# Three second products of the expert FFNs moved to other places in TensorE's order

## The chip, the cores and the metric

One core of a Trainium2 chip runs the whole program in one launch. The metric is the device time of that launch in microseconds (us). The engines are TensorE (PE; PEld is its weight load), VectorE (DVE), ScalarE (ACT), GpSimd (POOL) and SyncE (SP, which issues all DMAs). Each runs its own list of instructions in order and waits on semaphores for the others.

## The reference

The input x has 32 sequences of 256 tokens with 128 features, in fp32. Three layers follow one another, each on a layernorm of its input and added to it:

```python
x = x + 0.5 * ffn(layernorm(x))
x = x + mamba(layernorm(x))
x = x + 0.5 * ffn(layernorm(x))

# ffn: 8 experts, each token takes the one with the largest gate
idx = argmax(softmax(xf @ Wg + bg))
h = gelu(einsum('th,ehi->tei', xf, W1) + b1)     # exact gelu
y = einsum('tei,eih->teh', h, W2) + b2
out = y[token, idx[token]]

# mamba: rmsnorm, in_proj to 2 x 256, causal conv of 4 taps, silu,
# x_proj, dt = softplus(...), a scan over 256 steps with 16 states a channel
h = exp(dt * A) * h + (dt * x) * B ;  y = h . C
out = ((y + D * x) * silu(z)) @ out_proj + residual
```

## The kernel before

**Tiling.** The 8192 tokens are cut into 16 chunks of 512 (two sequences). A chunk goes through the first FFN (called f1, w = 0 in the code), the mamba layer (p) and the second FFN (f2, w = 1). The program is a software pipeline: iterations i = -4 to 18, each of 16 slots. In iteration i the scan works on chunk i, while other stages work on chunk i + off, with off from 4 (its load) to -3 (its store). Every engine has its own list that is written out by hand: tables name the slot, and a place within it, at which each step stands.

**The scan.** A slot handles two units of a chunk, so a chunk has 32. For a unit ACT makes the decay, an Exp into one of three PSUM banks dA (L632); DVE scans over time (L759, or L757 in slots 1, 3, 5, 9 and 14) and multiplies by C (L763; in those five slots POOL does it, L944); POOL makes dt*x*B (L936); PE sums the states into the bank Y (L489). A decay may be made only when the unit three before it has left its dA bank, that is after DVE's product (L763) or scan (L757) of that unit. ACT is one slot ahead: at slot 15 it makes the decays of units 0 and 1 of the next chunk.

**An FFN.** Only the chosen expert's values matter. For each expert e a first product puts xn @ W1 plus a bias that is very negative for tokens that chose another expert into the single PSUM bank PH (L461 in bf16, then L462 in fp32). ACT copies the bank into hs (L597, `take_first`); the next first product can start only after that copy. After the eighth, two gelus run over hs in place (L610, with a table load ahead, and one back at L614). Then for each e a second product adds hs @ W2 into the bank PY (`second_product`, L477: four matmuls of 128x128 in fp32, two records each in the trace; for e = 0 also a bias, L475). When all eight are in, DVE adds PY to X (L815, `add_to_x`), which frees PY for the other FFN.

**Where they stand.** `W1_AT` gives for each first product its slot and place on PE, its slot and place on ACT, and the chunk's offset; `W2_AT` gives slot, place and offset of each second product. On PE a slot runs: stages of place 0 and first products of place 0, stages of place 1, the state sum, then for k = 1, 2, 3 the first and then the second products of place k, then stages of place 2. Of f1, eight first products end in slot 15, the gelus follow on ACT at slot 15.5, and the second products of that chunk stand in slots 4 to 9 of the next iteration. DVE's add of f1 is at its place 10.0, and layernorm statistics for p follow at 10.5 (L738 to L744), POOL's roots (L881 to L901) at 11 and its normalization (L919) at 12, PE's transposes of that (L443) at slot 13, the projections x1 and x0 (L451) at slot 14. ACT's copy of the last but two first products, the taps of the convolution (L647) and DVE's part of it (L776) lie in slots 14 and 15. Of f2, the second products stand in slots 10 to 15; DVE's add of f2 is at place 1.5 of the next iteration. Slots 0 to 3 on PE hold the last state sum, the transposes of f1's layernorm (L443), three first products of f2, the gate (L531) and z0, z1 (L451); then comes the output projection (L511).

Of the kernel before, what the change touches and what calls it, by code (L numbers as in the profile page):

```python
# [68 lines left out]
         [(15, 1, 15, 0, -1), (15, 2, 15, 1, -1), (15, 3, 15, 3, -1), (1, 0, 0, 0, -2), (2, 0, 2, 0, -2),  # L69
          (3, 0, 3, 0, -2), (5, 0, 4, 2, -2), (6, 0, 6, 0, -2)]]  # L70

W2_AT = [[(s, 1, 2) for s in (4, 6, 8, 8, 8, 9, 9, 9)],
         [(s, k, -2) for s, k in ((10, 1), (11, 1), (12, 1), (13, 1), (14, 1), (14, 1), (15, 1), (15, 2))]]
W1_ORDER = sorted((s, k, w, e, off) for w in range(2) for e, (s, k, _, _, off) in enumerate(W1_AT[w]))
W1_TAKES = sorted((s, k, w, e, off) for w in range(2) for e, (_, _, s, k, off) in enumerate(W1_AT[w]))
W1_PLACE = {(w, e): n for n, (_, _, w, e, _) in enumerate(W1_ORDER)}
# [20 lines left out]
def w2_units(s, place):  # L97

    return [(w, e, off) for w in range(2) for e, (at, k, off) in enumerate(W2_AT[w]) if (at, k) == (s, place)]

# [930 lines left out]
```

## Time and profile before

| | us |
|---|---|
| median of 3 runs | 1493.84 (1493.03 to 1496.21) |
| the profiled execution's own time | 1495.2 |
| its span, first to last instruction | 1493.4 |
| PE busy | 1232.2 (83%) |
| POOL busy | 1067.6 (71%) |
| DVE busy | 1061.7 (71%) |
| ACT busy | 874.2 (59%) |
| mean granted TensorE clock | 0.849 of full |

The profiled execution took 1.8 us more than its span, and 1.4 us more than the median. In the middle of the program an iteration takes 82.4 us, and each engine has idle stretches in it at its own places; which engine is last changes within the iteration, so a busy share alone says little. The chain of waits follows the program back from its end through whatever was last at each step.

### The profile page before, as it was taken

What the parts mean: (1) busy time and instruction counts of PE and PEld (TensorE: products, weight loads), DVE (VectorE), ACT (ScalarE), POOL (GpSimd) and SP (SyncE); (2) the same over time, 40 slices, a digit from 0 to 9 for tenths busy, and PEclk for the clock granted to TensorE, in tenths of its full rate; (3) what the DMA queues carried; (4) which work ended last, traced back from release to release, by engine and by line L of the source; (5) the groups of instructions that cost most, each with busy time, mean ns of one, the idle gap of its engine ahead of it and who ended that gap; (6) DMA issues with size and microseconds to landing.
All of it is one profiled execution on the core that took longest, in us unless ns stands there. A gap on an engine that the chain in (4) does not pass through costs nothing.

```text
span 1493.4 us, 16302 instructions
## 1 busy us (share of the span) xinstructions
PE 1232.2 (83%) x5188; PEld 612.7 (41%) x5188; DVE 1061.7 (71%) x1713; ACT 874.2 (59%) x1171; POOL 1067.6 (71%) x900
## 2 busy tenths in 40 slices
PE   2777768889898989989898988899898978667677
PEld 1333314234443534445353444444353434333344
DVE  2022887887878787877878787878878776979910
ACT  0244656476666767575667667575756675474532
POOL 1026796978878788868788787878687886997600
PEclk9989876788888998888888889888888987978786
DMA  3005050413233231503232332305032322232000
GB/s 84 1 0 205 10 198 9 158 43 120 92 108 106 89 111 33 181 23 127 80 120 92 108 106 73 127 24 185 28 115 85 122 85 105 101 114 92 1 7 14
DMA packets 60405, 130.02 MB, mean 87 GB/s; under 512 B 7744, under 2 KB 26864, under 8 KB 52128
## 3 DMA queue, kind: packets, MB, share of 16 engines
q1 hardware_dynamic: 60320, 128.98, 25.1%
q8 instruction: 42, 0.69, 0.2%
q14 instruction: 43, 0.35, 0.1%
HBM read 106.94 MB, written 22.02 MB: 86 GB/s over the span
## 4 chain that ended last, share of the span: by engine, by line
PE 41%; ACT 24%; DVE 23%; issue 8%; POOL 3%; SPq 1%; ACTq 0%; DVEq 0%; DMA 0%; POOLq 0%
PE PH L462 12%; PE PY L477 9%; DVE dA L759 9%; PE G L451 9%; ACT hs L610 6%; ACT dA L632 5%; DVE hb L757 4%; ACT hs L597 4%; DVE hb L763 3%; PE PH L461 3%; ACT L614 3%; ACT L610 2%; PE Y L489 2%; PE G L511 2%; PE G L531 2%
## 5 line engine op out<-in xcount | busy, mean ns | idle before, releaser
L936 POOL TENSOR_TENSOR hb<-dtx_rep,bs 128x1024 f32<-128x1024 f32 x256 | 598.8, 2361 | 0.0
L759 DVE TENSOR_TENSOR_SCAN dA<-dA,hb 128x512 f32<-128x512 f32 x352 | 429.8, 1221 | 68.5 <-ACT dA L632 61.6
L632 ACT ACTIVATE dA<-dt_rep,A 128x512 f32<-128x512 f32 x512 | 342.2, 689 | 143.4 <-DVE hb L763 128.7
L597 ACT COPY hs<-PH 128x512 f32<-128x512 f32 x256 | 149.4, 584 | 388.2 <-PE PH L462 387.9
L462 PE MATMUL PH<-xnT,W 128*128 128x512 f32 x512 | 339.0, 749 | 0.0
L477 PEld LDWEIGHTS PY<-W,hs 128*128 128x128 f32 x2048 | 281.8, 208 | 101.2 <-issue 88.8
L477 PE MATMUL PY<-W,hs 128*128 128x128 f32 x2048 | 323.2, 304 | 0.0
L944 POOL TENSOR_TENSOR hb<-hb,cs 128x1024 f32<-128x1024 f32 x80 | 188.4, 2355 | 140.7 <-DVE hb L757 140.7
L763 DVE TENSOR_TENSOR hb<-dA,cs 128x512 f32<-128x512 f32 x352 | 243.5, 692 | 25.2 <-DVE dA L759 0.9
L757 DVE TENSOR_TENSOR_SCAN hb<-dA,hb 128x512 f32<-128x512 f32 x160 | 186.3, 1206 | 102.6 <-ACT dA L632 99.5
L489 PE MATMUL Y<-hb,Sel 128*32 128x512 f32 x1024 | 164.5, 716 | 19.8 <-POOL hb L944 10.4
L461 PE MATMUL PH<-ohT,Lm 24*128 24x512 bf16 x256 | 109.1, 426 | 83.4 <-ACT hs L597 82.7
L610 ACT ACTIVATE hs<-hs 128x2048 f32<-128x2048 f32 x64 | 121.3, 1909 | 0.4
L462 PEld LDWEIGHTS PH<-xnT,W 128*128 128x128 f32 x512 | 86.6, 212 | 68.3 <-issue 68.3
L461 PEld LDWEIGHTS PH<-ohT,Lm 24*128 24x128 bf16 x256 | 23.5, 92 | 219.7 <-ACT hs L597 147.0
L776 DVE SCALAR_TENSOR_TENSOR xs<-G,Wc,xs 128x506 f32<-128x506 f32 (+2 forms) x96 | 67.2, 742 | 65.0 <-ACT xs L647 62.7
L531 PE MATMUL G<-Wg,xnT 128*128 128x8 f32 x256 | 56.2, 348 | 64.2 <-ACT xnT L590 64.2
L881 POOL TENSOR_SCALAR neg<-mv 128x4 f32<-128x4 f32 x48 | 9.7, 203 | 127.3 <-DVE mv L744 127.3
L963 POOL TENSOR_TENSOR dt<-dt,sp 128x1024 f32<-128x1024 f32 x16 | 37.6, 2353 | 83.5 <-ACT sp L676 83.5
L531 PEld LDWEIGHTS G<-Wg,xnT 128*128 128x128 f32 x256 | 53.8, 309 | 94.3 <-ACT xnT L590 94.0
L489 PEld LDWEIGHTS Y<-hb,Sel 128*32 128x32 f32 x1024 | 22.7, 116 | 114.1 <-issue 86.6
L815 DVE SCALAR_TENSOR_TENSOR X<-PY,X 128x512 f32<-128x512 f32 x32 | 21.8, 682 | 60.8 <-PE PY L477 60.8
(85 smaller groups left out, 1190.7 us busy)
## 6 DMA issues: line engine op xcount, KB each, us to landing
dtx_rep<-dtx_rows SPq DMA_DIRECT2D x32, 1024.0 KB, 6.5
dt_rep<-dt_rows SPq DMA_DIRECT2D x32, 1024.0 KB, 8.2
bs<-bc_rows SPq DMA_DIRECT2D x64, 256.0 KB, 3.7
cs<-bc_rows SPq DMA_DIRECT2D x64, 256.0 KB, 4.5
dtx_rows<-dtx SPq DMA_DIRECT2D x32, 256.0 KB, 2.5
dt_rows<-dt SPq DMA_DIRECT2D x32, 256.0 KB, 2.6
X<-in_x SPq DMA_DIRECT2D x16, 256.0 KB, 3.0
out<-X SPq DMA_DIRECT2D x16, 256.0 KB, 2.4
```

Source lines behind the costliest of these rows:

```text
L461: nc.tensor.matmul(PH[:, :], Lm[:, e, :], ohT[:, w, :], start=True, stop=False)
L462: nc.tensor.matmul(PH[:, :], W1[:, e, :], xnT[:, w, :], start=False, stop=True).then_inc(ph_full, 1)
L477: last = nc.tensor.matmul(PY[:, P * j:P * (j + 1)], hs[:, w, e, P * j:P * (j + 1)], W2[:, e, :], start=False, stop=e == E - 1 and j == J - 1)
L489: last = nc.tensor.matmul(Y[D32 * g:D32 * (g + 1), :], Sel[:, :], hb[:, (2 * k + g // 2) % HR, g % 2], start=q == 0, stop=q == NQ - 1)
L597: nc.scalar.copy(hs[:, w, e, :], PH[:, :]).then_inc(ph_free, 1)
L610: nc.scalar.activation(a, a, ACT.Gelu).then_inc(gelu[w], 1)
L632: nc.scalar.activation(dA[u % NA][:, :], dt_rep[:, h, g, :], ACT.Exp, scale=A[:, h, g, q:q + 1]).then_inc(decay, 1)
L757: nc.vector.tensor_tensor_scan(x_in_hb, a, x_in_hb, 0.0, ALU.mult, ALU.add).then_inc(scan, 1)
L759: nc.vector.tensor_tensor_scan(a, a, x_in_hb, 0.0, ALU.mult, ALU.add).then_inc(scan, 1)
L763: nc.vector.tensor_tensor(x_in_hb, a, cs[:, q, :], ALU.mult).then_inc(prod, 1)
L936: nc.gpsimd.tensor_tensor(hb[:, s % HR], dtx_rep[:, h, 2 * m:2 * m + 2, :], bs[:, q, None, :].broadcast_to([P, 2, CH]), ALU.mult).then_inc ...
L944: nc.gpsimd.tensor_tensor(hb[:, s % HR], hb[:, s % HR], cs[:, q, None, :].broadcast_to([P, 2, CH]), ALU.mult).then_inc(prod_p, 1)
```

## The change

One table changes. It holds for each expert of each FFN the slot, the place and the chunk offset of its second product.

```diff
-W2_AT = [[(s, 1, 2) for s in (4, 6, 8, 8, 8, 9, 9, 9)],
-         [(s, k, -2) for s, k in ((10, 1), (11, 1), (12, 1), (13, 1), (14, 1), (14, 1), (15, 1), (15, 2))]]
+W2_AT = [[(s, k, 2) for s, k in ((4, 1), (6, 1), (8, 1), (8, 1), (8, 1), (9, 1), (9, 1), (9, 3))],
+         [*[(s, 1, -2) for s in (10, 11, 12, 13, 14, 15)], (0, 1, -3), (1, 1, -3)]]
```

Of f2, experts 0 to 3 stay. Slot 14 held two second products (4 and 5) and slot 15 two more (6 and 7); now slot 14 holds expert 4, slot 15 expert 5, and experts 6 and 7 stand in slots 0 and 1 of the next iteration. Of f1, expert 7 moves within slot 9 from ahead of a first product to behind it. No instruction is added or removed, and no engine but PE has another order; the semaphores count on.

PE from x0 (L451) in slot 14 to the last first product of slot 15, in the middle of the program, before. L451 is a projection, L477 second products, L461 with L462 a first product, L489 the state sum:

```order
L451 MATMUL G0<-xrT,Win 128x512
L477 MATMUL PY<-W2,hs 128x128 x8
L461 MATMUL PH<-ohT,Lm 128x512
L462 MATMUL PH<-xnT,W1 128x512
L489 MATMUL Y<-hb,Sel 32x512 x4
L461 MATMUL PH<-ohT,Lm 128x512
L462 MATMUL PH<-xnT,W1 128x512
L477 MATMUL PY<-W2,hs 128x128 x4
L461 MATMUL PH<-ohT,Lm 128x512
L462 MATMUL PH<-xnT,W1 128x512
L477 MATMUL PY<-W2,hs 128x128 x4
L461 MATMUL PH<-ohT,Lm 128x512
L462 MATMUL PH<-xnT,W1 128x512
```

and now:

```order
L451 MATMUL G0<-xrT,Win 128x512
L477 MATMUL PY<-W2,hs 128x128 x4
L461 MATMUL PH<-ohT,Lm 128x512
L462 MATMUL PH<-xnT,W1 128x512
L489 MATMUL Y<-hb,Sel 32x512 x4
L461 MATMUL PH<-ohT,Lm 128x512
L462 MATMUL PH<-xnT,W1 128x512
L477 MATMUL PY<-W2,hs 128x128 x4
L461 MATMUL PH<-ohT,Lm 128x512
L462 MATMUL PH<-xnT,W1 128x512
L461 MATMUL PH<-ohT,Lm 128x512
L462 MATMUL PH<-xnT,W1 128x512
```

Four matmuls of L477 (one second product) are gone ahead of the first PH pair, and no L477 stands any more between the last two pairs.

PE from the last state sum (slot 0) to the gate (L531, slot 2), before:

```order
L489 MATMUL Y<-hb,Sel 32x512 x4
L443 MATMUL G0<-Id,xn 128x128 x4
L461 MATMUL PH<-ohT,Lm 128x512
L462 MATMUL PH<-xnT,W1 128x512
L461 MATMUL PH<-ohT,Lm 128x512
L462 MATMUL PH<-xnT,W1 128x512
L531 MATMUL G1<-Wg,xnT 128x8 x4
```

and now:

```order
L489 MATMUL Y<-hb,Sel 32x512 x4
L477 MATMUL PY<-W2,hs 128x128 x4
L443 MATMUL G0<-Id,xn 128x128 x4
L461 MATMUL PH<-ohT,Lm 128x512
L462 MATMUL PH<-xnT,W1 128x512
L477 MATMUL PY<-W2,hs 128x128 x4
L461 MATMUL PH<-ohT,Lm 128x512
L462 MATMUL PH<-xnT,W1 128x512
L531 MATMUL G1<-Wg,xnT 128x8 x4
```

One second product now stands ahead of the transposes L443, another between the two first products.

PE in slot 9 and on to the gate of f2, before:

```order
L443 MATMUL G1<-Id,xn 128x128 x4
L489 MATMUL Y<-hb,Sel 32x512 x4
L477 MATMUL PY<-W2,hs 128x128 x12
L461 MATMUL PH<-ohT,Lm 128x512
L462 MATMUL PH<-xnT,W1 128x512
L461 MATMUL PH<-ohT,Lm 128x512
L462 MATMUL PH<-xnT,W1 128x512
L531 MATMUL G0<-Wg,xnT 128x8 x4
```

and now:

```order
L443 MATMUL G1<-Id,xn 128x128 x4
L489 MATMUL Y<-hb,Sel 32x512 x4
L477 MATMUL PY<-W2,hs 128x128 x8
L461 MATMUL PH<-ohT,Lm 128x512
L462 MATMUL PH<-xnT,W1 128x512
L477 MATMUL PY<-W2,hs 128x128 x4
L461 MATMUL PH<-ohT,Lm 128x512
L462 MATMUL PH<-xnT,W1 128x512
L531 MATMUL G0<-Wg,xnT 128x8 x4
```

The last of the three second products of slot 9 now follows the first product.

## Rows read from the trace of the kernel before

**Rows 1.** The page: busy time, share of the span, instructions of each engine.

```profile
PE 1232.2 (83%) x5188; PEld 612.7 (41%) x5188; DVE 1061.7 (71%) x1713; ACT 874.2 (59%) x1171; POOL 1067.6 (71%) x900
```

**Rows 2.** Chain of waits, slots 14 to 0: start us, us, what.

```profile
705.52 1.78 PE PY L477 x16
...
711.05 0.89 PE PY L477 x8
...
713.40 0.59 ACT hs L597
```

**Rows 3.** Timeline of ACT, same place: start, duration, what, [idle before, releaser].

```profile
712.02 0.69 ACT L632 ACTIVATE dA<-dt_rep,A 128x512 f32<-128x512 f32 x1 [0.30 <-DVE hb L763]
713.40 0.59 ACT L597 COPY hs<-PH 128x512 f32<-128x512 f32 x1 [0.69 <-PE PH L462]
713.89 0.70 ACT L632 ACTIVATE dA<-dt_rep,A 128x512 f32<-128x512 f32 x1
```

**Rows 4.** Timeline of DVE, slots 14 to 1.

```profile
707.27 2.72 DVE L776 SCALAR_TENSOR_TENSOR xs<-G,Wc,xs 128x506 f32<-128x506 f32 x4 [2.65 <-ACT xs L647]
...
713.10 0.69 DVE L763 TENSOR_TENSOR hb<-dA,cs 128x512 f32<-128x512 f32 x1
...
725.45 0.68 DVE L815 SCALAR_TENSOR_TENSOR X<-PY,X 128x512 f32<-128x512 f32 x1
```

**Rows 5.** Timeline of DVE, then of ACT, where chunk 2's scan begins.

```profile
301.05 0.69 DVE L763 TENSOR_TENSOR hb<-dA,cs 128x512 f32<-128x512 f32 x1
...
301.78 0.69 ACT L632 ACTIVATE dA<-dt_rep,A 128x512 f32<-128x512 f32 x1 [0.60 <-DVE hb L763]
```

**Rows 6.** Timeline of PE, slots 0 to 4.

```profile
718.34 0.38 PE L461 MATMUL PH<-ohT,Lm 24*128 24x512 bf16 x1 [1.18 <-ACT hs L597]
...
722.04 0.60 PE L461 MATMUL PH<-ohT,Lm 24*128 24x512 bf16 x1 [2.27 <-ACT hs L597]
...
735.46 2.02 PE L511 MATMUL G<-Wo,y 128*128 128x128 f32 x16
```

**Rows 7.** Windows: us, busy (count) of PE, PEld, DVE, ACT, POOL; granted clock.

```profile
717.00:721.50 4.50, 1.60 (x5) 0.39 (x3) 2.43 (x3) 4.47 (x5) 2.65 (x2) 1.00 0.00 0
722.00:735.00 13.00, 12.48 (x26) 4.11 (x26) 11.78 (x17) 8.20 (x13) 8.03 (x4) 0.50 0.14 40
```

**Rows 8.** Timeline of PE, then DVE, slots 9 and 10.

```profile
757.22 2.94 PE L477 MATMUL PY<-W,hs 128*128 128x128 f32 x24
...
763.18 0.39 PE L461 MATMUL PH<-ohT,Lm 24*128 24x512 bf16 x1 [1.64 <-ACT hs L597]
...
764.87 0.68 DVE L815 SCALAR_TENSOR_TENSOR X<-PY,X 128x512 f32<-128x512 f32 x1
```

**Rows 9.** Timeline of PE, DVE, POOL, iteration -1.

```profile
134.01 0.66 PE L443 MATMUL G<-Id,xr 128*128 128x128 f32 x4
...
125.94 0.69 DVE L815 SCALAR_TENSOR_TENSOR X<-PY,X 128x512 f32<-128x512 f32 x1 [12.48 <-PE PY L477]
...
132.21 1.75 POOL L919 TENSOR_SCALAR xr<-X,neg,rms 128x128 f32<-128x128 f32 x4
```

**Rows 10.** Timeline of DVE, iteration 0.

```profile
185.81 0.68 DVE L815 SCALAR_TENSOR_TENSOR X<-PY,X 128x512 f32<-128x512 f32 x1
187.66 1.23 DVE L759 TENSOR_TENSOR_SCAN dA<-dA,hb 128x512 f32<-128x512 f32 x1 [1.18 <-ACT dA L632]
```

**Rows 11.** Timeline of POOL, iteration 1.

```profile
273.81 0.20 POOL L881 TENSOR_SCALAR neg<-mv 128x4 f32<-128x4 f32 x1 [0.61 <-DVE mv L744]
```

**Rows 12.** Timeline of DVE, chunk 15's second unit pair.

```profile
1363.05 2.34 DVE L757 TENSOR_TENSOR_SCAN hb<-dA,hb 128x512 f32<-128x512 f32 x2 [0.87 <-ACT dA L632]
```

**Rows 13.** Timeline of PE, iteration 13, where the output projection ran at the low clock.

```profile
1227.82 3.75 PE L511 MATMUL G<-Wo,y 128*128 128x128 f32 x16 [4.12 <-ACT zs L655]
```

**Rows 14.** Chain of waits: the second dt copy of iteration 13, and of iteration 7.

```profile
1247.65 0.69 ACT dt L668
...
749.86 0.69 ACT dt L668
```

## The prediction

> **What bounds the kernel now.** I read the page first. PE is busy for 83% of the span and DVE and POOL for 71% [rows 1], so no engine is full, and the order within an iteration decides. Next the chain of waits, in the middle of the program, where an iteration takes 82.4 us. From slot 14 on it runs over PE, through the second products that the change touches (two of them in 1.78 us, one in 0.89), and leaves for ACT's copy of a first product at 713.40 [rows 2]. Taken alone this says: each second product less ahead of that copy is worth 0.89 us in each iteration. The reader should look at what ACT does after the copy, and at what else it waits for there. After the copy comes the decay of unit 1 at 713.89 [rows 3]. It needs its dA bank back, from a product that DVE began at 713.10 and that takes 0.69 us: free at 713.79 [rows 4]. DVE is thus 0.10 us behind PE as the cause. Where DVE alone is last, at the start of chunk 2, the product ends at 301.05 + 0.69 = 301.74 and the decay starts at 301.78, 0.04 us later [rows 5]. Then the timelines of the engines: where they are idle, and what ends it.
>
> **Slots 14 and 15, removed.** Of the products that leave, one (0.89 us, [rows 2]) stood ahead of the first product whose copy the chain takes, the other behind it. PE gets there 0.89 us sooner. ACT then has only the decay of unit 0 ahead, which DVE frees at 712.02 [rows 3] and the change does not move. The copy starts at about 712.6, and the decay of unit 1 at 713.79 + 0.04 = 713.83 instead of 713.89: 0.06 us, in eleven iterations 0.7 us. DVE itself does not come sooner: its work in these slots hangs on the convolution's taps, for which it was idle 2.65 us [rows 4], and these need only x1, x0 and a copy that all stand ahead of the removed product. Next late after PE is DVE, at once. Bounds of this term: 0.04 us of gain an iteration, and 0.89 if my reading of the bank is wrong (first rival).
>
> **Slots 0 and 1, added.** PE waits for ACT's copies there 1.18 us, and then 2.27 us [rows 6]. The product of expert 6 takes the time that was given free ahead, so the transposes and the next first product (718.34) stand where they were. That of expert 7 starts at about 719.7 and ends at 720.6 at the full clock, ahead of the first product at 722.04. At half the clock (16 such records in 3.75 us, [rows 13]) it takes 1.88 and ends at 721.6, still ahead. Then DVE's add of f2 at 725.45 [rows 4] has its eighth product 4.8 us early. Price: nothing. Without the cover, where no gelu keeps ACT busy, each would cost 0.89.
>
> **Slot 9.** In the middle of the program PE finishes the three second products (2.94 us for three, [rows 8]) and the first product behind them by 761.5, and waits for ACT until 763.18. The exchange leaves both in that stretch; the eighth product ends at 761.5 instead of 760.1, and DVE adds f1 at 764.87 [rows 8]. Nothing. At the start there are no gelus of f2 at that place, and two effects show. (a) DVE's add waits for the eighth product itself: idle 12.48 us until 125.94 [rows 9]. It now comes one first product later, about 1.37 us. Its statistics and POOL's roots follow, POOL's normalization from 132.21 for 1.75 us, and PE's transposes at 134.01 [rows 9] begin as that ends. Iteration -1 loses about 1.3. Iteration -2 has the same path; I take 0.8 for it, between nothing and 1.3. (b) In iterations 0 and 1 DVE waits on ACT behind that first product: idle 1.18 until 187.66 [rows 10]. The first product is done 0.89 sooner; the add (185.81, 0.68 us) moves back by some 0.4, and DVE gains 0.8. In iteration 1 the path goes on over POOL, which had waited only 0.61 us [rows 11]: gain 0.6. Together 1.3 + 0.8 - 0.8 - 0.6 = 0.7 us lost. Bounds: a gain of 1.4 if only (b) holds, a loss of 2.1 if only (a).
>
> **The end.** No f1 is left there, so no gelu covers slots 0 and 1. At the start of chunk 15, DVE was already idle 0.87 us behind ACT [rows 12], and ACT behind a first product that now has the product of expert 6 ahead: 0.8 lost. In iteration 15 PE and ACT alternate on first products and their copies. Expert 6 between the state sum and the next first product costs 0.89 there; in iteration 16 one second product less stands ahead of the first of these and the others fill waits for copies, some 0.75 gained. Together 0.9 lost; bounds 0 and 2.6.
>
> **The sum.** Measured against the profiled execution: -0.7 + 0.7 + 0.9 = +0.9, so 1495.2 becomes 1496.1. This execution took 1.4 us more than the median of the runs (1493.84), so the forecast is 1494.7. A measurement of this kernel can tell about 0.2%, 3 us, from no change.
>
> **The clock.** The windows show PE 1.60 of 4.50 us busy at the full clock, and right behind it 13 us at a granted clock of 0.50, that is 1.2 GHz of 2.4 [rows 7]. The low stretch ends about where the output projection starts at 735.46, which takes 2.02 us for 16 records [rows 6], nearly twice the 0.89 for 8 at the full clock. So the low clock costs nothing now: the path there is DVE's. The product of expert 7 falls into the idle stretch that precedes the fall. The Trainium skill (TensorE: Matmul & The Clock Gate, what's actually happening) says that throttled is the default and that activity lifts it. By that rule added work there delays the fall. The trace agrees on the order, idle and then low; for how much work suffices it has no row.
>
> **Rivals.**
> 1. *The chain as written.* PE, not DVE, holds the decay of unit 1: 0.89 us in eleven iterations, 9.8 us, less the 1.6 lost at the ends: 1494.7 - 9.1 = 1485.6. For it speaks the chain of waits, which names PE and ACT; against it the 0.04 us of [rows 5] beside the 0.10 here. Or the ends turn out well: expert 6 and 7 between the last first products keep the clock up there, an estimated microsecond each for two or three. Chance of faster by over 0.2%: 0.15.
> 2. *The low clock moves onto the critical stretch.* The fall comes later, and the low stretch reaches past 735.46, over the output projection, the first second products, B, C and dt, where PE sets the pace. One iteration shows the price: in iteration 13 the projection took 3.75 us [rows 13] from 1227.82, and ACT's second dt copy came at 1247.65, 19.83 us after its start. In iteration 7 that is 749.86 - 735.46 = 14.40 [rows 6, 14]. So at most 5.4 us an iteration, 60 us in eleven: 1554. It decides from the point where the low stretch ends behind the start of the projection. Against it: in the low stretch PE is busy 12.48 of 13 us [rows 7] with work that starts when ACT is ready, and stays where it is, so the rise should come where it came. I take four iterations of eleven at two thirds of the price: 14 us, 1508. Chance of slower by over 0.2%: 0.25, with smaller shifts and a loss of 3 us at the ends in it.
> 3. *The change doesn't do what it says*: it does; PE's order shows the three moves and no other.
>
> **How the numbers follow.** No change 0.60, faster 0.15, slower 0.25. The forecast's own range is 1491.5 to 1497. The range for 8 in 10 takes in half of each rival's side: 1488 to 1506.
>
> **What would show it.** Right: the decay of unit 1 follows DVE's product by 0.04 us, iterations stay at 82.3 to 82.4, PE's wait of 1.18 stays, that of 2.27 shrinks to about 1.4, a new one of some 0.9 stands in slot 15, DVE's add of f1 in iteration -1 comes 1.4 us later, in the middle everything stands as before. Wrong: iterations of 81.5 us (rival 1), or a granted clock of 0.50 between the output projection and dt (rival 2).

## The result, and the profile after

The changed kernel takes 1510.3 us (median of 4 runs, 1505.45 to 1511.29); the kernel before took 1493.43 beside it (4 runs, 1492.01 to 1496.21). The ratio is 1.0104, with a 95% interval of 1.0078 to 1.0131: slower by 1%. The forecast was 1494.7 with a range to 1506. Rival 2 had 1508, for a reason that turned out to be about half of it. One of the ten executions of e11 below took 2091.06 us; it is left out of that kernel's ratio, but its median of 1496.04 has it in (1495.47 without it).

The page of the kernel after, busy time of each engine, beside [rows 1]:

```profile
PE 1226.6 (81%) x5188; PEld 613.8 (41%) x5188; DVE 1062.3 (70%) x1713; ACT 874.1 (58%) x1171; POOL 1066.5 (71%) x900
```

The work is the same. PE is even 5.6 us less busy in a span that is 15.6 us longer (1509.0 instead of 1493.4, granted clock 0.859 instead of 0.849). So the sums of busy time don't show the loss, nor does the mean clock, which is higher than before; where the low clock falls has to be looked up stretch by stretch. To do that I cut each span where ACT begins the decay (L632) of a chunk's unit 1. The profiled executions give:

| stretch, us | before | after | difference |
|---|---|---|---|
| start to unit 1 of chunk 0 | 145.01 | 155.97 | +10.96 |
| chunk 0 to chunk 2 | 156.77 | 154.66 | -2.11 |
| chunk 2 to chunk 12, ten iterations | 824.89 | 832.80 | +7.91 |
| chunk 12 to chunk 15 | 231.75 | 230.56 | -1.19 |
| chunk 15 to the end | 134.98 | 135.0 | 0.0 |

**The middle: two iterations of eleven.** Most iterations take 82.35 us, 0.06 less than before. Timelines of DVE and ACT of the kernel after, the counterpart of [rows 3, 4] (start, duration, what, [idle before, releaser]):

```profile
726.10 0.69 DVE L763 TENSOR_TENSOR hb<-dA,cs 128x512 f32<-128x512 f32 x1
```

```profile
725.02 0.69 ACT L632 ACTIVATE dA<-dt_rep,A 128x512 f32<-128x512 f32 x1 [1.20 <-DVE hb L763]
725.65 0.58 ACT L597 COPY hs<-PH 128x512 f32<-128x512 f32 x1
726.82 0.69 ACT L632 ACTIVATE dA<-dt_rep,A 128x512 f32<-128x512 f32 x1 [0.60 <-DVE hb L763]
```

The product ends at 726.10 + 0.69 = 726.79 and the decay of unit 1 starts at 726.82, 0.03 behind it. ACT's copy is early now, and ACT waits 0.60 us for DVE. That is the forecast's reading of the bank.

But iterations 3 and 9 take 86.86 and 86.85 us. Timeline of PE of the kernel after from slot 15 to the projection, first in iteration 7, a usual one:

```profile
726.28 0.38 PE L461 MATMUL PH<-ohT,Lm 24*128 24x512 bf16 x1 [0.87 <-ACT hs L597]
...
734.97 0.39 PE L461 MATMUL PH<-ohT,Lm 24*128 24x512 bf16 x1 [1.38 <-ACT hs L597]
...
738.06 1.88 PE L531 MATMUL G<-Wg,xnT 128*128 128x8 f32 x8 [1.65 <-ACT xnT L590]
...
748.39 2.02 PE L511 MATMUL G<-Wo,y 128*128 128x128 f32 x16 [2.34 <-ACT zs L655]
```

and in iteration 3:

```profile
404.14 1.06 PE L531 MATMUL G<-Wg,xnT 128*128 128x8 f32 x8 [1.65 <-ACT xnT L590]
...
414.47 2.53 PE L511 MATMUL G<-Wo,y 128*128 128x128 f32 x16 [2.98 <-ACT zs L655]
...
417.15 0.80 PE L477 MATMUL PY<-W,hs 128*128 128x128 f32 x2
```

The windows of the same iteration 3 (us, busy (count) of PE, PEld, DVE, ACT, POOL; granted clock, DMA share, GB/s):

```profile
400.00:405.50 5.50, 2.80 (x12) 1.58 (x13) 3.88 (x5) 5.08 (x9) 1.40 (x1) 1.00 0.00 0
405.50:409.20 3.70, 3.70 (x9) 0.74 (x11) 3.53 (x6) 0.69 (x1) 3.70 (x3) 0.54 0.52 142
409.20:415.80 6.60, 3.38 (x22) 1.68 (x18) 6.14 (x10) 5.21 (x8) 4.73 (x3) 1.00 0.01 2
415.80:426.00 10.20, 10.20 (x35) 4.84 (x34) 6.68 (x17) 4.35 (x6) 8.38 (x8) 0.50 0.00 1
```

The reader is to see two low stretches between unit 1 and dt, where the kernel before had one [rows 7]. (Both kernels have a further one later in the iteration; it is not at issue here.) In the kernel before the low stretch of iteration 7 began 7.7 us after unit 1 (721.6 - 713.89). With the product of expert 7 ahead it begins 9.9 us after it in iteration 7 (736.7 - 726.82) and 12.7 in iteration 3 (405.6 - 392.90), where even the gate L531 still runs at full clock (1.06 us instead of 1.88). The clock is back at 1.00 by 409.2. PE is then done early with little work, waits 2.98 us for ACT's z, and the granted clock falls again at 415.8, just as the output projection has begun. The projection itself is not late: it starts 21.57 us after unit 1 in iteration 3 as in iteration 7 and in the kernel before (735.46 - 713.89). From here on PE sets the pace: two records of a second product take 0.80 us (0.49 in iteration 7), and the rest up to 426.0 runs at 1.2 GHz too. ACT's dt copies come at 430.76 and 433.37, that is 40.47 us after the decay of unit 1 for the second of them; in iteration 7 it is 762.78 - 726.82 = 35.96. The difference is 4.5 us, and it is the whole difference of the iteration. The same holds for all profiles of this case: from iteration 3 to 10 the projection takes 2.02 to 2.07 us behind a wait of 2.41 us or less, and 2.51 to 2.85 us behind a wait of 2.98 us, and it is these iterations, and no others, that take 86.9 us.

**The start.** The first add of f1 that is exposed, then the second, in the timeline of DVE, beside [rows 9]; and PE between them:

```profile
81.77 0.69 DVE L815 SCALAR_TENSOR_TENSOR X<-PY,X 128x512 f32<-128x512 f32 x1 [10.51 <-PE PY L477]
...
134.43 0.69 DVE L815 SCALAR_TENSOR_TENSOR X<-PY,X 128x512 f32<-128x512 f32 x1 [16.07 <-PE PY L477]
```

```profile
86.33 1.13 PE L462 MATMUL PH<-xnT,W 128*128 128x512 f32 x2
89.80 0.66 PE L443 MATMUL G<-Id,xr 128*128 128x128 f32 x4 [2.35 <-POOL xr L919]
...
93.21 2.08 PE L451 MATMUL G<-xrT,Win 128*128 128x512 f32 x2 [1.22 <-ACT xrT L590]
...
95.75 2.08 PE L462 MATMUL PH<-xnT,W 128*128 128x512 f32 x2
```

The same place in the kernel before, timeline of PE:

```profile
86.42 1.80 PE L462 MATMUL PH<-xnT,W 128*128 128x512 f32 x2
88.00 1.06 PE L443 MATMUL G<-Id,xr 128*128 128x128 f32 x4
...
92.16 1.12 PE L451 MATMUL G<-xrT,Win 128*128 128x512 f32 x2 [1.22 <-ACT xrT L590]
...
93.53 1.12 PE L462 MATMUL PH<-xnT,W 128*128 128x512 f32 x2
```

Here PE went from the first product to the transposes without a wait. The clock was low for a short time, from 86.7 to 90.1 (the transposes took 1.06 us), and then high until 100.4. Now the add of f1 in iteration -2 comes at 81.77 instead of 79.69, POOL's normalization follows it, and PE waits 2.35 us for POOL. The transposes start at 89.80 instead of 88.00, 1.8 us later; 0.7 of that was there ahead of the exchange (a first product at 76.25 instead of 75.53). They still run at the full clock, but at 91.5 it falls and stays low until 98.4: the same matmuls take 2.08 us instead of 1.12. Windows over the start, after and then before (columns as above):

```profile
92.00:100.00 8.00, 6.79 (x10) 2.16 (x10) 0.78 (x2) 3.01 (x5) 2.73 (x5) 0.60 0.00 0
...
112.00:125.00 13.00, 13.00 (x36) 5.68 (x35) 0.41 (x1) 5.11 (x7) 0.00 (x0) 0.61 0.03 7
```

```profile
92.00:100.00 8.00, 4.73 (x10) 1.45 (x10) 3.80 (x6) 5.04 (x7) 0.79 (x2) 1.00 0.00 0
...
112.00:125.00 13.00, 13.00 (x73) 8.60 (x73) 0.41 (x1) 6.74 (x9) 2.27 (x1) 1.00 0.12 26
```

In the last window PE is busy without a break in both kernels, at 1.00 before and 0.61 after, and gets through 73 records before and 36 after (some of them larger ones). The next low stretch is longer too, 105.2 to 122.3 instead of 100.4 to 110.6, and so is the one behind it, 139.3 to 153.0 instead of 137.9 to 141.3. The loss of 11 us builds up so: the gate of f1 in iteration -2 starts at 108.04 instead of 104.54 (3.5); from there to the add of f1 it takes 26.4 us instead of 21.4 (5.0, of them 1.4 for the first product that the exchange put ahead, the rest is the clock); and from the add to chunk 0's unit 1 21.54 instead of 19.07 (2.5).

### The profile page after: what moved, and what is told of

The parts are those of the page before. It is cut to its first block, busy times and chain, and to the rows that moved or that the text cites. A ratio compares the mean times of both kernels' runs of the same rounds, so it can differ in the third digit from the quotient of the medians.

```text
span 1509.0 us, 16302 instructions
## 1 busy us (share of the span) xinstructions
PE 1226.6 (81%) x5188; PEld 613.8 (41%) x5188; DVE 1062.3 (70%) x1713; ACT 874.1 (58%) x1171; POOL 1066.5 (71%) x900
## 4 chain that ended last, share of the span: by engine, by line
PE 31%; DVE 30%; ACT 23%; issue 10%; POOL 4%; SPq 1%; DVEq 0%; ACTq 0%; DMA 0%; POOLq 0%
DVE dA L759 12%; PE PH L462 8%; PE G L451 7%; PE PY L477 6%; ACT hs L610 6%; ACT dA L632 5%; DVE hb L763 5%; DVE hb L757 5%; ACT hs L597 3%; PE G L511 2%; PE PH L461 2%; DVE xs L776 2%; ACT L614 2%; PE Y L489 2%; ACT L610 2%
## 5 line engine op out<-in xcount | busy, mean ns | idle before, releaser
L632 ACT ACTIVATE dA<-dt_rep,A 128x512 f32<-128x512 f32 x512 | 342.6, 689 | 174.9 <-DVE hb L763 153.6
L477 PEld LDWEIGHTS PY<-W,hs 128*128 128x128 f32 x2048 | 287.3, 209 | 122.7 <-issue 110.0
L462 PE MATMUL PH<-xnT,W 128*128 128x512 f32 x512 | 331.6, 734 | 0.0
L477 PE MATMUL PY<-W,hs 128*128 128x128 f32 x2048 | 331.5, 306 | 0.0
L489 PE MATMUL Y<-hb,Sel 128*32 128x512 f32 x1024 | 164.9, 717 | 28.0 <-POOL hb L944 15.3
L461 PE MATMUL PH<-ohT,Lm 24*128 24x512 bf16 x256 | 108.3, 423 | 76.6 <-ACT hs L597 76.1
L462 PEld LDWEIGHTS PH<-xnT,W 128*128 128x128 f32 x512 | 85.6, 210 | 67.4 <-issue 67.4
L531 PE MATMUL G<-Wg,xnT 128*128 128x8 f32 x256 | 52.0, 332 | 73.7 <-ACT xnT L590 73.6
L461 PEld LDWEIGHTS PH<-ohT,Lm 24*128 24x128 bf16 x256 | 23.5, 92 | 197.3 <-ACT hs L597 125.4
L531 PEld LDWEIGHTS G<-Wg,xnT 128*128 128x128 f32 x256 | 49.0, 286 | 97.8 <-ACT xnT L590 97.8
L489 PEld LDWEIGHTS Y<-hb,Sel 128*32 128x32 f32 x1024 | 22.9, 116 | 121.4 <-issue 87.7
```

The costliest lines, as they stand in the source:

```text
L461: nc.tensor.matmul(PH[:, :], Lm[:, e, :], ohT[:, w, :], start=True, stop=False)
L462: nc.tensor.matmul(PH[:, :], W1[:, e, :], xnT[:, w, :], start=False, stop=True).then_inc(ph_full, 1)
L477: last = nc.tensor.matmul(PY[:, P * j:P * (j + 1)], hs[:, w, e, P * j:P * (j + 1)], W2[:, e, :], start=False, stop=e == E - 1 and j == J - 1)
L489: last = nc.tensor.matmul(Y[D32 * g:D32 * (g + 1), :], Sel[:, :], hb[:, (2 * k + g // 2) % HR, g % 2], start=q == 0, stop=q == NQ - 1)
L632: nc.scalar.activation(dA[u % NA][:, :], dt_rep[:, h, g, :], ACT.Exp, scale=A[:, h, g, q:q + 1]).then_inc(decay, 1)
```

## Experiments

The ratio is of each kernel to the kernel before in the same rounds. The same kernel varies by up to 12 us between executions (before: 1485.63 to 1497.75 in 31); a profile shows one of them. So profiles are compared here by stretches. Chunk 0's unit 1 stands at 144.7 to 147.5 us in the eight profiled kernels whose start is that of the kernel before. Where a kernel's profiled execution is far from its median, this is said.

### Each part alone

**e1_f1_only**: only the exchange in slot 9 (the first changed line of the diff).

> Only the exchange in slot 9 (f1, expert 7 behind the first product); f2 as before. Theory A (the exchange costs at the start: DVE's add of f1 comes later in iterations -2 and -1, PE idles ahead of the transposes of the p layer and runs at the low clock after it): chunk 0's unit 1 starts 9 to 11 us later than the 145.0 us of before, the middle has iterations of 82.4 us as before, total 1502 to 1505. Rival B (all of the loss comes from the f2 part): total within 2 us of before, 1493.

Measured: 1501.24 us (before 1494.93), ratio 1.0038 (1.0012 to 1.0065). Chunk 0's unit 1 at 156.97, iterations 3 to 10 at 82.41, iteration 11 at 84.31 (83.12 before). The exchange costs at the start what the whole change costs there, a little more than expected, and nothing in iterations 3 to 10.

**e2_f2_only**: only the three moves of f2 (the second changed line).

> Only the f2 part (experts 5, 6, 7 in slots 15, 0 and 1); f1 as before. Theory A: the start is as before (unit 1 of chunk 0 at about 145 us), iterations take 82.35 us but for some (2 of 11 in the changed kernel) with 4.5 us more, in which the low-clock stretch reaches past the output projection; total 1497 to 1503. Rival B: 1508 to 1511. Rival C (nothing in the middle, that was chance): 1493 to 1494.

Measured: 1501.01 us, ratio 1.0045 (1.0025 to 1.0066). Chunk 0's unit 1 at 147.24. Iteration 5 takes 86.87 us, its second dt copy again 40.47 after unit 1, and iteration 11 takes 84.19; the others from 3 to 10 take 82.35. Iteration 11 can't be put down to this move, since e1 has 84.31 there without it. From chunk 12 to 15 it takes 230.82 us.

**e5_f1_from_2**: the exchange in slot 9 from iteration 2 on.

```diff
                         for unit in w2_units(s, k):
-                            second_product(it, *unit)
+                            if (s, k) != (9, 3) or it.i0 >= 2:
+                                second_product(it, *unit)
+                        if (s, k) == (9, 1) and it.i0 < 2:
+                            second_product(it, 0, 7, 2)
```

> The exchange in slot 9 from iteration 2 on only; iterations -2 to 1 and all of f2 are as before. Theory A (the f1 part costs only at the start, where DVE's add waits for the eighth product itself): no loss, 1492 to 1496, unit 1 of chunk 0 at about 145 us. Rival (it costs in the middle too): 1498 or more.

Measured: 1492.6 us (before 1492.64), ratio 0.9997 (0.9984 to 1.0011). The exchange is free wherever the gelus of f2 stand; what it costs, it costs in the iterations before 2.

**e10_f2_chunks_to_10** and **e11_f2_chunks_from_11**: the moves of f2 for the first eleven chunks alone, or for the last five alone. The first of them (the other has `chunk >= 11`):

```diff
+            def moved(chunk):
+                return chunk <= 10
...
-                        for unit in w2_units(s, k):
-                            second_product(it, *unit)
+                        for w, e, off in w2_units(s, k):
+                            if w == 0 or e < 5 or not moved(it.i0 + off):
+                                second_product(it, w, e, off)
+                        for at, e, off in ((15, 5, -2), (0, 6, -3), (1, 7, -3)):
+                            if (s, k) == (at, 1) and moved(it.i0 + off):
+                                second_product(it, 1, e, off)
```

> The move of the three second products of f2 for chunks 0 to 10 alone; chunks 11 to 15 and f1 stand as before. Theory (in the middle the product of expert 7 in PE's idle stretch puts the fall of the clock off, and in some iterations it then falls a second time ahead of the output projection, 4.5 us each, while 0.06 us is gained in each): one to three iterations of 86.9 us between chunks 3 and 11, all others 82.35, and from chunk 12 on the spans of the kernel before: in all +2 to +8 us, 1495 to 1501. Rival (the loss of f2's move comes from the end alone): no iteration over 82.7, 0.5 us faster than before.

Measured: 1499.87 us (before 1492.69), ratio 1.0049 (1.0030 to 1.0068). Iteration 5 takes 86.85 us and iteration 11 84.15, the others 82.33 to 82.35 up to there; behind them iteration 13 takes 82.46 with its second dt copy at 38.63 instead of 35.68, as it also happens in the kernel before. The rival (loss from the end alone) is out. The loss is as large as that of e2, where f2 is moved for all chunks (1.0045).

> The move of the three second products of f2 for chunks 11 to 15 alone; chunks up to 10 and f1 stand as before. Theory (at the end the product of expert 6 stands ahead of a first product that ACT waits for, and one product less in slot 14 leaves PE idle and its clock low): everything as before until chunk 11, then 0 to 4 us slower, 1493 to 1497; DVE waits over 1 us for ACT's decay at the start of chunk 14 or 15. Rival (the loss comes from the middle alone; at the end the first products at full clock gain as much as expert 6 costs): 1488 to 1493.

Measured: 1496.04 us, ratio 1.0018 (0.9990 to 1.0046): the interval holds 1, so the time alone doesn't decide. The trace does: the middle stands as before, and iteration 14 takes 70.73 us, where the nine profiled kernels with the old order at the end have 66.9 to 69.0 (e12 not counted, which adds work there). Timeline of DVE and PE in e11, where chunk 14's scan begins:

```profile
1296.22 2.34 DVE L764 TENSOR_TENSOR_SCAN hb<-dA,hb 128x512 f32<-128x512 f32 x2 [1.27 <-ACT dA L639]
```

```profile
1288.43 0.38 PE L461 MATMUL PH<-ohT,Lm 24*128 24x512 bf16 x1 [1.66 <-ACT hs L604]
1288.74 1.81 PE L462 MATMUL PH<-xnT,W 128*128 128x512 f32 x2
1290.48 1.94 PE L489 MATMUL Y<-hb,Sel 128*32 128x512 f32 x8
1292.35 1.20 PE L477 MATMUL PY<-W,hs 128*128 128x128 f32 x8
1293.48 0.38 PE L461 MATMUL PH<-ohT,Lm 24*128 24x512 bf16 x1
```

and the same place in e8 (below), which has the old order here:

```profile
1284.55 0.38 PE L461 MATMUL PH<-ohT,Lm 24*128 24x512 bf16 x1
1284.86 1.12 PE L462 MATMUL PH<-xnT,W 128*128 128x512 f32 x2
1285.92 1.06 PE L489 MATMUL Y<-hb,Sel 128*32 128x512 f32 x8
1286.91 0.39 PE L461 MATMUL PH<-ohT,Lm 24*128 24x512 bf16 x1
```

From one first product to the next it is 2.36 us in e8 and 5.05 in e11. Of these 2.69, the product of expert 6 takes 1.13; the rest is the low clock behind a wait of 1.66 us, in L462 (0.69 more) and in L489 (0.88 more). The wait is for a copy of ACT that itself comes no later than in e8. PE is there sooner, since one second product less stands in slot 14, and the one that stood between these two first products (1283.56 in e8, 1.05 us) is gone.

**e3_f2_both_in_slot0**: the moves of f2 with experts 6 and 7 both in slot 0, so that none stands in the idle stretch.

```diff
-         [(s, k, -2) for s, k in ((10, 1), (11, 1), (12, 1), (13, 1), (14, 1), (14, 1), (15, 1), (15, 2))]]
+         [*[(s, 1, -2) for s in (10, 11, 12, 13, 14, 15)], (0, 1, -3), (0, 1, -3)]]
```

> As e2, but experts 6 and 7 of f2 both in slot 0; between the two first products of slots 1 and 2 PE is idle again as before. If the product in that idle stretch is what moves the low-clock stretch, no iteration of the middle takes over 83 us here, and the total is 1493 to 1496. If it is the work taken from slots 14 and 15, it is as e2.

Measured: 1496.17 us, ratio 1.0032 (1.0009 to 1.0055). No iteration of the middle over 82.7 us in the profiled execution (1495.8), and chunk 12 to 15 in 230.3. Its runs reach from 1492.8 to 1502.9, so this one profile doesn't show that the others had no long iteration. It fits the theory and doesn't prove it. Nor do the ratios: the intervals of e2 and e3 overlap.

### The clock alone

**e4_idle_filled_before**: the kernel before, no product moved; four matmuls of 128x128 are added where the change put expert 7. Their result is not read.

```diff
                         first_product(it, *unit)
+                    if s == 1 and it.has(0):
+                        it.wait_free(pe, g_free, "gate_f1")
+                        for j in range(J):
+                            nc.tensor.matmul(G[1][:, P * j:P * (j + 1)], W1[:, 7, :], W2[:, 7, :],
+                                             start=True, stop=True)
```

> The kernel before, with four matmuls of 128x128 more in slot 1 of every iteration from 0 on, written to the bank of the gate ahead of the gate, which overwrites them. They lie in the idle stretch in which expert 7 lies in the changed kernel, and no table is changed. Theory A (activity there moves the low-clock stretch): some iterations of the middle have 4.5 us more, total 1498 to 1504. If it is the order of the second products and not PE's activity: 1493 to 1494.

Measured: 1498.86 us, ratio 1.0040 (1.0018 to 1.0061). Iterations 5 and 10 take 86.9 us. Windows of iteration 5 of this kernel:

```profile
560.80:564.20 3.40, 3.40 (x5) 0.60 (x3) 3.26 (x4) 0.69 (x1) 3.40 (x3) 0.50 0.55 154
564.20:571.00 6.80, 3.58 (x21) 1.61 (x21) 6.31 (x12) 5.02 (x7) 4.94 (x3) 1.00 0.00 1
571.00:581.30 10.30, 10.30 (x36) 5.21 (x36) 6.70 (x16) 4.53 (x7) 8.31 (x7) 0.50 0.01 2
```

This is iteration 3 of the changed kernel again, with nothing moved and nothing needed in the added work; the projection starts 21.58 us after unit 1 as elsewhere. So the 4.5 us come from the clock, and work in the idle stretch is enough to bring them about.

**e6_f1_start_filled**: e1 with eight matmuls more ahead of the transposes for p in iterations -2 and -1, in the wait for POOL. Their result is overwritten.

```diff
                 if now("ln_p"):
+                    if it.i0 in (-2, -1):
+                        it.wait_free(pe, g_free, "ln_p")
+                        fill(G[G_AT["ln_p"][0]], 8)
                     it.wait(pe, xr_ready, 2, 1, 1)
...
+            def fill(bank, n):
+                for j in range(n):
+                    nc.tensor.matmul(bank[:, P * (j % J):P * (j % J + 1)], W1[:, 7, :], W2[:, 7, :],
+                                     start=True, stop=True)
```

> As e1 (the f1 part alone), with eight matmuls of 128x128 more ahead of the p layer's transposes in iterations -2 and -1, in the stretch in which PE waits for POOL there (2.35 us in the changed kernel). They write a bank that the transposes overwrite. If most of the 11 us at the start is the low clock that follows this stretch: unit 1 of chunk 0 at 147 to 150 us, total 1493 to 1497. If it is the direct delay of DVE's add and what follows: as e1, 156 to 157 us, or later, total 1501.

Measured: 1490.8 us (before 1492.64), ratio 0.9987 (0.9976 to 0.9999), where e1 had 1.0038: some 7.5 us. Chunk 0's unit 1 stands at 144.55 instead of 156.97, in an execution that was 5 us faster than the median. Timeline and windows of this kernel at the start:

```profile
86.51 1.95 PE L553 MATMUL G<-W 128*128 128x128 f32 x16
89.03 0.66 PE L443 MATMUL G<-Id,xr 128*128 128x128 f32 x4 [0.57 <-POOL xr L928]
```

```profile
92.00:100.00 8.00, 4.73 (x10) 1.45 (x10) 3.68 (x6) 5.04 (x7) 1.97 (x5) 1.00 0.00 0
...
112.00:125.00 13.00, 13.00 (x72) 8.48 (x71) 0.41 (x1) 6.87 (x9) 2.26 (x1) 1.00 0.09 26
```

The exchange is still there, and so is its direct delay; the wait of 2.35 has become 0.57, the clock stays at 1.00 until 100.3, and the loss is gone. So most of the loss at the start goes with the low clock. How much exactly isn't shown: time and unit 1 are both better than expected, and the fill may gain something in the kernel before too, which no run tried alone. A hint is e9 below, which has such fill in addition to that of e8, with unit 1 at 139.42 instead of 142.77.

### A kernel that beats both

**e7_end_filled**: the kernel before with fill in iteration 17 (bank Y is idle there): two matmuls ahead of each of the last five first products, sixteen during the last gelus. **e8_start_filled**: the kernel before with two matmuls ahead of each first product of f1 in iteration -3 but the first two.

```diff
                     for unit in w1_units(s, 0):
+                        if it.i0 == -3:
+                            fill(PY, 2)
+                        if it.i0 == NCH + 1 and unit[0] == 1:
+                            fill(Y, 2)
                         first_product(it, *unit)
                     stages(it, s, 1)
+                    if it.i0 == NCH + 1 and s == 10:
+                        fill(Y, 16)
```

(e8 has the first addition, e7 the two others. The loop also passes the five places of f2's first products, where iteration -3 has none yet. So e8, e9 and e12 hold five pairs more, ten matmuls ahead of the first first product; the expectation below doesn't name them.)

> The kernel before, with matmuls in PE's waits of iteration 17: two of 128x128 ahead of each of the last five first products, 16 while the last gelus run. They write the bank Y, which nobody reads any more. If the low clock of the end is worth what its rows say (last first products 2.6 instead of 1.4 us, second products 12.4 instead of 7.1 us for 32): 1484 to 1490. If the clock doesn't answer to them: 1494 to 1496.

Measured: 1487.32 us (before 1492.64), ratio 0.9962 (0.9948 to 0.9976); from chunk 15's unit 1 to the end 128.8 us instead of 134.98.

> The kernel before, with two matmuls of 128x128 ahead of each first product of iteration -3 but the first two, in PE's waits for ACT's copies, where the clock was low. They write the bank PY, unused until iteration -2. If activity lifts the clock there: unit 1 of chunk 0 at 138 to 142 us instead of 145, total 1487 to 1492. If not: each costs 0.2 us, 1495.

Measured: 1487.44 us (before 1492.64), ratio 0.9967 (0.9951 to 0.9983); chunk 0's unit 1 at 142.77, a little behind the expected 138 to 142. The first products of iteration -3 start 1.4 us later (32.67 instead of 31.28), behind the added pairs, and from the fourth on they run at the full clock: 1.12 us in L462 instead of 2.08.

**e9_start_and_end_filled**: both, and four matmuls ahead of the transposes as in e6.

> The kernel before, with added matmuls of 128x128 that nobody reads (their banks are overwritten afterwards) in three places: 4 ahead of the transposes for p in iterations -2 and -1, 2 ahead of each first product of f1 in iteration -3, and in iteration 17 the 2 ahead of the last five first products and 16 during the last gelus. No work of the kernel is moved. Theory (the low clock on the critical stretches at start and end is what costs time, and each stretch is separate): e7 gained 5.3 to 6 us at the end and e8 5.2 us at the start, so the two together gain 10 to 12 us, 1481 to 1484, ratio 0.992 to 0.994; the fill ahead of the transposes adds 0 to 2 more, since the kernel before ran them at full clock. Chunk 0's second decay stands at 142 to 144 us, and the time from chunk 15's second decay to the end is some 5 us shorter than 135. Rival (a rise at one place is paid by a fall at another, since added work only shifts the low stretches): less than the sum, 1486 to 1489.

Measured: 1480.58 us (1478.94 to 1481.28; before 1492.69), ratio 0.9922 (0.9897 to 0.9946): faster than the kernel before by 12 us and than the changed one by some 30. Chunk 0's unit 1 stands at 139.42, sooner than expected; from chunk 15's unit 1 to the end it takes 129.25 us. The last part of the kernel before, timeline of PE:

```profile
1468.07 2.08 PE L462 MATMUL PH<-xnT,W 128*128 128x512 f32 x2
...
1477.53 0.26 PE L475 MATMUL PY<-b_part,ohT 24*128 24x128 bf16 x1 [4.04 <-ACT hs L610]
...
1480.54 9.43 PE L477 MATMUL PY<-W,hs 128*128 128x128 f32 x58
```

and of e9, where L553 is the fill:

```profile
1459.53 0.39 PE L461 MATMUL PH<-ohT,Lm 24*128 24x512 bf16 x1 [0.29 <-ACT hs L612]
1459.84 1.12 PE L462 MATMUL PH<-xnT,W 128*128 128x512 f32 x2
1460.80 3.73 PE L553 MATMUL Y<-W 128*128 128x128 f32 x32
...
1466.88 6.74 PE L477 MATMUL PY<-W,hs 128*128 128x128 f32 x58
```

The 58 records of the last products take 6.74 us instead of 9.43, and the last first product 1.12 instead of 2.08 in L462; so it is for the two ahead of it.

**e12_out_filled_too**: e9 and twelve matmuls ahead of the output projection from iteration 13 on.

```diff
                 if now("out"):
+                    if it.i0 >= 13:
+                        it.wait(pe, y_added[1], -3, 1, 1)
+                        fill(PY, 12)
```

> As the run with start and end filled, and 12 more added matmuls of 128x128 ahead of the output projection in iterations 13 to 15, into the bank of the second products while it is free. Nobody reads them. Theory (in the kernel before the projection of iteration 13 took 3.75 us instead of 2.02 since PE had waited 4.12 us at the low clock, and what follows is as slow; work in that wait raises the clock): the projection takes 1.8 to 2.1 us in all three, and 1 to 5 us are gained on the run with start and end filled, 1477 to 1482. Rival (the path there is ACT's or DVE's, and the added matmuls, up to 0.12 us each at the low clock, delay z and the projection): 0 to 3 us slower than that run.

The addition stands in iteration 16 too, which the expectation leaves out, and a matmul is two records: at the low clock (16 records in 3.75 us, [rows 13]) one takes 0.47 us, not 0.12.

Measured: 1480.57 us, ratio 0.9927 (0.9899 to 0.9955), the same as e9. The projection takes 2.02 us in iterations 13 and 14 and 1.95 in 15. Iterations 13 and 14 gained 1.5 us each (dt at 34.14 instead of 35.68 and 28.11 instead of 29.71). It was given back in iteration 15: there the projection comes 13.94 us after unit 1 instead of 11.27, behind 2.94 us of fill at a place where PE had waited for nothing. So the theory held in iterations 13 and 14, and in 15 the fill was pure delay.

## Why the prediction was wrong, point by point

- **Slots 14 and 15: right.** 82.35 instead of 82.41 us, DVE's product last with 0.03 us to the decay. Rival 1, the chain as written, is out: a chain of waits named PE, and 0.89 us less on PE brought 0.06.
- **Slots 0 and 1: right for the direct cost.** The waits are 1.02 and 1.38 us (1.18 and 2.27 in [rows 6]; the forecast had 1.18 and 1.4), the one in slot 15 0.87. Relative to unit 1, DVE adds f2 at 11.56 us in both kernels.
- **Slot 9 in the middle: right.** The add of f1 stands 50.98 us after unit 1 in both kernels; e5 gives a ratio of 0.9997.
- **Slot 9 at the start: wrong, the largest miss.** Forecast 0.7 us lost, bounds -1.4 to 2.1; measured 10.96 - 2.11 = 8.9 lost in the profiles. Part (b), the gain in iterations 0 and 1, is 2.1 in these profiles (forecast 1.4). In iteration 0 it came as forecast: DVE's idle 1.18 us of [rows 10] is gone, 0.51 behind PE is new, and the iteration is 0.6 shorter. The rest can't be told from chance, since kernels with the old start took 152.7 to 159.1 us from chunk 0 to 2. Part (a) priced only the delay itself, 1.3 and 0.8. What failed is the step that took everything behind the delayed add to last as long as before. The delay turned into a wait of PE of 2.35 us at a place where PE had run through, the granted clock fell behind it, and PE sets the pace in what follows. The rival on the clock was looked for in the middle only. e6 bears it out: with the wait filled, the same exchange brings no loss; what share of that is the fill's own gain stays open.
- **The clock in the middle: rival 2, right in what is hit, not in how.** The forecast itself took the low clock to cost nothing, and this step failed. The rival has one low stretch that starts later and reaches past the projection. It does start later, but it ends earlier: 16.7 us after unit 1 in iteration 7 (743.5 - 726.82) instead of 21.4 (735.3 - 713.89). This by itself costs nothing. The cost is a second fall, in the wait ahead of the output projection, which the forecast did not have. It was to be seen in the iteration 13 that gave the price: the clock was at 1.00 from 1220.5 to 1226.0, and low again from 1228.0 on. Two iterations at 4.5 us measured, four at 3.6 forecast for the rival: 9 instead of 14. e2, e4 and e10 each show such iterations at the same price, at other places of the program.
- **The end: 0.9 lost forecast, with bounds to 2.6; not settled.** Two things work against each other in the profiles. Iteration 14 takes 70.6 to 70.9 us in the four kernels with f2 moved there (after, e2, e3, e11) and 66.9 to 69.0 in the nine with the old order: some 3 us lost, by the product of expert 6 and by the low clock behind PE's new wait, which the term did not have. Iteration 13 takes 78.3 to 78.4 us in the four. In the nine it takes 78.4 to 78.5 four times, and five times 81.4 to 83.4, as in the kernel before (82.50, [rows 13]), where the low stretch lasts until 1240.4; after, it ends with the projection, at 1248.7. From chunk 12 to 15 the four take 230.6 us on average and the nine 229.9. Whether the move spares iteration 13 the long low stretch or four profiles had luck, no run here shows. The times don't settle it either: e10 without the move at the end costs as much as e2 with it (1.0049 and 1.0045), and the interval of e11 holds 1, but e3 is slower (1.0032) with no long iteration in its profile. The part behind chunk 15 came out at 0.
- **The sum.** +10.96 - 2.11 + 7.91 - 1.19 = +15.6 us of span. From the parts run alone, medians and ratios give 5.7 us for f1 and 6.7 for f2; the whole change gives 15.5. That the two together cost more than their sum, by 3 us, is within the intervals, and I did not settle whether it is more.

What stays open: in which iterations the clock falls a second time. In the profiled executions it was 3 and 9 in the changed kernel, 5 in e2 and e10, and 5 and 10 in e4, with the same order of the program in all iterations from 3 to 10. No run here explains the choice.

The Trainium skill (TensorE: Matmul & The Clock Gate, A second HAM failure mode: psum-queue depth-cycling) tells of a kernel that cycles through PSUM banks and where short idle times between groups of matmuls made the clock swing between its two levels. The traces here agree as to the short idle times: in the window from 400.0 PE was busy 2.80 of 5.50 us, with waits of 1.38 and 1.65 us and a first product between them, and the clock fell behind them.

## What to carry to other kernels

Before a product is moved out of or into PE's idle time, ask of each wait of PE what runs behind it: if PE's work after the wait is on the critical path, the direct delay can be the smaller part. Here a wait of 2.35 us where there had been none came with 9 us of loss. The place to look is wherever PE is nearly idle just ahead of a stretch in which it sets the pace, above all at the start and the end of a pipeline. Where such a wait can't be avoided, matmuls whose results nobody reads are worth trying: in three places here they gained 0.8% together, and in a fourth, where PE had not waited, they cost what they took.

## What was unexpected of the hardware

- Added work on PE in an idle stretch made the kernel slower without delaying anything directly (e4: four matmuls of 128x128 an iteration, +0.4%), and at other places made it faster (e9: -0.8%). The loss sits where the low stretch lies on work that PE paces.
- The clock fell behind waits of 0.73 to 1.65 us each where several stood in a row between short pieces of work. In the kernel before, the last first products alternate with waits of 0.73 us for ACT's copies, and the last three of them and the second products behind them, up to 1486.2, ran at 0.50.
- The same program differed by up to 12 us between executions of its own (before: 1485.6 to 1497.8 in 31 runs beside e1 to e4). The traces show one source of such differences: in nine kernels with the same order there, iteration 13 took 78.4 to 78.5 us or 81.4 to 83.4, by how long the low stretch at its projection lasted. Whether this makes up the 12 us isn't shown.
